# Cross-attention over 12544 keys: block maximum in two VectorE instructions, value matmuls in two halves

## The reference

```python
K = (K_in @ Wk + bk).reshape(b, l, NH, DK).transpose(0, 2, 1, 3)
V = (V_in @ Wv + bv).reshape(b, l, NH, DK).transpose(0, 2, 1, 3)
Q = (Q_in @ Wq + bq).reshape(b, lp, NH, DK).transpose(0, 2, 1, 3)
KQ = jnp.einsum('bhld,bhpd->bhlp', K, Q) / np.float32(np.sqrt(DK))
KQ = KQ + mask_pad.reshape(b, 1, l, 1)
KQ = KQ + mask_attn.T.reshape(1, 1, l, lp)
alpha = jax.nn.softmax(KQ, axis=2)
O = jnp.einsum('bhlp,bhld->bhpd', alpha, V)
O = O.transpose(0, 2, 1, 3).reshape(b, lp, NH * DK)
return O @ Wo + bo
```

## Time and profile before

| | before |
|---|---|
| median of 3 runs | 2421.47 us (2418.22 to 2424.6) |
| profiled execution | 2424.6 us |
| its span | 2422.8 us |
| granted TensorE clock over the span | 0.958 |
| TensorE matmul busy | 2268.4 us (94%) |
| weight loads busy | 1892.1 us (78%) |
| VectorE busy | 1584.7 us (65%) |
| ScalarE busy | 1504.9 us (62%) |
| GpSimd busy | 413.6 us (17%) |

### The profile page before, as it was taken

The page is one execution under the profiler, slowest core; times in us unless marked ns, Lnnn a source line. Parts: engine busy times, 40 slices in busy tenths (PEclk is TensorE's granted clock), DMA queues, the critical chain, the costliest instruction groups (busy, mean ns, idle before and its releaser), DMA issues. The chain is left out here.

```text
span 2422.8 us, 68489 instructions
## 1 busy us (share of the span) xinstructions
PE 2268.4 (94%) x26863; PEld 1892.1 (78%) x26863; DVE 1584.7 (65%) x3621; ACT 1504.9 (62%) x3044; POOL 413.6 (17%) x353
## 2 busy tenths in 40 slices
PE   7999999988999999999877999999967999999968
PEld 6888888777788788787755888888856888888758
DVE  4777777635777777777653777777735777777532
ACT  2666666634788788887523666666633666666611
POOL 3211222002221221220002122222003222212000
PEclk7999999998999999999888999999988999999969
DMA  6677666475444344341155766666517666776345
GB/s 131 116 126 126 118 115 122 61 222 149 100 118 125 99 123 115 104 119 40 46 179 117 123 107 116 116 116 117 77 52 144 121 121 121 124 125 112 49 132 173
DMA packets 152460, 279.62 MB, mean 115 GB/s; under 512 B 32829, under 2 KB 72078, under 8 KB 152218
## 3 DMA queue, kind: packets, MB, share of 16 engines
q1 hardware_dynamic: 148842, 272.18, 54.5%
q10 hardware_dynamic: 3376, 4.03, 0.7%
HBM read 120.94 MB, written 0.33 MB: 50 GB/s over the span
## 5 line engine op out<-in xcount | busy, mean ns | idle before, releaser
L1143 DVE TENSOR_REDUCE L2x_tops<-L2x_m_bank 128x1 f32<-128x448 f32 x448 | 262.5, 618 | 130.4 <-PE L2x_m_bank L907 128.2
L1143 DVE TENSOR_REDUCE L0x_tops<-L0x_m_bank 128x1 f32<-128x448 f32 x448 | 262.5, 618 | 129.7 <-PE L0x_m_bank L907 127.4
L1143 DVE TENSOR_REDUCE L3x_tops<-L3x_m_bank 128x1 f32<-128x448 f32 x448 | 262.5, 618 | 127.6 <-PE L3x_m_bank L907 125.4
L559 DVE CUSTOM_DVE_ANT_0 L1x_p_s<-L1x_p_s,L1x_mask,L1x_neg_max 128x512 f32<-128x512 f32 (+1 forms) x400 | 288.8, 743 | 57.2 <-PE L1x_p_s L320 54.7
L452 ACT ACTIVATE L1x_prob<-L1x_p_s,L1x_neg_max 128x512 f32<-128x512 f32 (+1 forms) x400 | 274.9, 687 | 68.8 <-DVE L1x_neg_max L559 66.9
L1042 ACT ACTIVATE L3x_prob<-L3x_s_bank 128x512 f32<-128x512 f32 x448 | 219.6, 542 | 90.8 <-PE L3x_s_bank L918 89.4
L1042 ACT ACTIVATE L0x_prob<-L0x_s_bank 128x512 f32<-128x512 f32 x448 | 219.6, 542 | 90.3 <-PE L0x_s_bank L918 89.2
L1042 ACT ACTIVATE L2x_prob<-L2x_s_bank 128x512 f32<-128x512 f32 x448 | 219.6, 542 | 87.8 <-PE L2x_s_bank L918 86.5
L329 PE MATMUL L1x_p_t<-net_ident,L1x_prob 128*128 128x128 f32 x1568 | 240.5, 275 | 13.7 <-ACT L1x_probT L174 11.5
L329 PEld LDWEIGHTS L1x_p_t<-net_ident,L1x_prob 128*128 128x128 f32 x1568 | 192.7, 141 | 57.1 <-ACT L1x_probT L174 23.6
L320 PE MATMUL L1x_p_s<-L1x_k_stack,L1x_q_stack 96*128 96x512 f32 (+1 forms) x400 | 182.5, 458 | 1.9 <-DVE L1x_q_stack L542 1.9
(11 more groups left out here) (766 smaller groups left out, 4469.9 us busy)
## 6 DMA issues: line engine op xcount, KB each, us to landing
L0x_k_stack<-L0x_kT SPq DMA_DIRECT2D x333, 112.0 KB, 4.1
L2x_k_stack<-L2x_kT SPq DMA_DIRECT2D x333, 112.0 KB, 4.0
L3x_k_stack<-L3x_kT SPq DMA_DIRECT2D x333, 112.0 KB, 4.0
L1x_k_stack<-L1x_kT SPq DMA_DIRECT2D x288, 128.0 KB, 2.4
L3f_w<-in_L_ffn_w SPq DMA_DIRECT2D x16, 1024.0 KB, 7.8
L0f_w<-in_L_ffn_w SPq DMA_DIRECT2D x48, 256.0 KB, 5.2
L1x_ctx<-in_ctxT SPq DMA_DIRECT2D x24, 512.0 KB, 3.9
L0x_ctx<-in_ctxT SPq DMA_DIRECT2D x13, 896.0 KB, 6.3
```

What stands on the lines that cost most here:

```text
L559: e.tensor_tensor_reduce(s, s, mask[:, odd, 0:nk], -1.0, neg_max[:, 1 - odd, h:h + 1], ALU.add, ALU.min, neg_max[:, odd, h:h + 1]).then_in ...
L1143: e.tensor_reduce(tops[:, b % 2, h, half:half + 1], m_bank[n % RING][:, 0:HALF], AX, ALU.max).then_inc(sem("m_free"), 1)
```

## The change

The block's maximum of a head is now made in two VectorE instructions. The first adds the mask in place, not negated, and reduces by maximum into a new tile `block_max`, with a constant as start value. The second, on one element per partition, waits for the first one's result, negates it and takes the minimum with the running value of the block before. It alone signals `maxed`. The exponential loses its scale of -1. Three waits per head (and one per block) that stood before the old instruction are gone, with one of its two registers.

`values` takes a half: the first half of a group's matmuls (key tiles 0 and 1 of 4) is issued nine steps behind, the second ten steps behind, in the step after. The waits stand before the first half only, and the signal `valued` is given after the second.

```diff
-VALUE_LAG = 9
+VALUE_LAGS = (9, 10)
@@ TensorE
-            def values(b, odd, g):
+            def values(b, odd, g, half):
                 nk = keys(b)
-                if g == 0:
+                nt = nk // P // 2
+                if half == 0 and g == 0:
                     e.wait_ge(sem("proj_copied"), (b + 1) * 4)
-                    if not (isinstance(b, int) and b == 0):
-                        e.wait_ge(sem("oT_copied"), b)
+                if half == 0 and g == 0 and not (isinstance(b, int) and b == 0):
+                    e.wait_ge(sem("oT_copied"), b)
                 last_of = {copied(h): h for h in range(4 * g, 4 * g + 4)}
-                for h in last_of.values():
+                for h in last_of.values() if half == 0 else ():
                     e.wait_ge(sem(copied(h)), copies(b, h))
-                for t in range(nk // P):
+                for t in range(half * nt, half * nt + nt):
...
-                i.then_inc(sem("valued"), 1)
+                if half == 1:
+                    i.then_inc(sem("valued"), 1)
...
-                at = lagging(b, odd, step, VALUE_LAG)
-                if at and at[2] % 4 == 0:
-                    values(at[0], at[1], at[2] // 4)
+                for half, lag in enumerate(VALUE_LAGS):
+                    at = lagging(b, odd, step, lag)
+                    if at and at[2] % 4 == 0:
+                        values(at[0], at[1], at[2] // 4, half)
@@ ScalarE
                     e.activation(prob[:, h % P_RING, 0:nk], p_s[h % S_RING][:, 0:nk], ACT.Exp,
-                                 bias=neg_max[:, odd, h:h + 1], scale=-1.0).then_inc(sem("exped"), 1)
+                                 bias=neg_max[:, odd, h:h + 1]).then_inc(sem("exped"), 1)
@@ VectorE
-                e.wait_ge(sem("mask_made"), b + 1)
+                if mask_kind:
+                    e.wait_ge(sem("mask_made"), b + 1)
                 for h in range(HX):
-                    made, raised = in_register(e, b * HX + h + 1), in_register(e, (b - 1) * HX + h + 1)
-                    e.wait_ge(sem("acc_zero"), 2)
-                    if not first:
-                        e.wait_ge(sem("maxed"), raised)
-                        if h == 0:
-                            e.wait_ge(sem("stepped"), b)
+                    made = in_register(e, b * HX + h + 1)
+                    if mask_kind:
+                        e.wait_ge(sem("acc_zero"), 2)
                     e.wait_ge(sem("scored"), made)
                     s = p_s[h % S_RING][:, 0:nk]
-                    e.tensor_tensor_reduce(s, s, mask[:, odd, 0:nk], -1.0, neg_max[:, 1 - odd, h:h + 1], ALU.add, ALU.min,
-                                           neg_max[:, odd, h:h + 1]).then_inc(sem("maxed"), 1)
+                    if mask_kind:
+                        e.tensor_tensor_reduce(s, s, mask[:, odd, 0:nk], 1.0, -3e38, ALU.add, ALU.max,
+                                               block_max[:, h:h + 1]).then_inc(sem("head_maxed"), 1)
+                    else:
+                        e.tensor_reduce(block_max[:, h:h + 1], s, AX, ALU.max).then_inc(sem("head_maxed"), 1)
+                    e.wait_ge(sem("head_maxed"), b * HX + h + 1)
+                    e.scalar_tensor_tensor(neg_max[:, odd, h:h + 1], block_max[:, h:h + 1], -1.0,
+                                           neg_max[:, 1 - odd, h:h + 1], ALU.mult, ALU.min).then_inc(sem("maxed"), 1)
```

More of the change, by code:

```diff
@@ L110, in cross_attention @@
     mask = sb("mask", [P, 2, KB]) if mask_kind else None
+    block_max = sb("block_max", [P, HX])
     neg_max = sb("neg_max", [P, 2, HX])
```

## The result

The changed kernel takes 2452.14 us (median of 4 runs, 2446.27 to 2457.81), the kernel before on the same chip 2419.84 (4 runs, 2413.66 to 2424.6). The ratio is 1.0135, interval 1.0108 to 1.0162: slower by 32.3 us, where +22 was forecast. It lies in the stated range, 2430 to 2461, but above the +16 to +29 that the prediction gave to its own mechanism, among the totals of its rival 2.

What follows compares the result with a forecast made beforehand. TensorE was taken to set the pace, with a chain through VectorE in B. Per block -0.21 + 0.50 + 0.64 = +0.93 us, x 24 = +22.3 us, hence 2444 us on the median; range 2430 to 2461.

Steps and rivals of the forecast that it cites:

- its own mechanism: The split and the two-part maximum lengthen TensorE's sequence: +22.3 us in all, range +16 to +29, chance 0.60.
- rival 2: VectorE becomes the bound: +1.43 us per block, +34 us in all; chance 0.15.
- -0.21 + 0.64 + a covered 0.32: Split of values, us per block: A shortens 0.21, C grows 0.64, B's added 0.32 is covered by VectorE's chain.
- A: Part of TensorE's block period from scores of head 0 to turn(1): 8.18 us before, forecast 7.97.
- C: Part of TensorE's block period from turn_out to the next block's first scores: 10.43 us before, forecast 11.07.
- +0.50 in B: In B, heads 5 and 6 each take VectorE 0.25 us longer with the maximum in two instructions.
- B: Part of TensorE's block period from turn(1) to turn_out, a chain through VectorE: 4.27 us before, forecast 4.77.
- reductions of 0.69: Sign that the prediction is wrong: VectorE's reductions fall to 0.69 us from 0.75.
- The 0.53: TensorE's wait in A before the turn of step 4, behind ScalarE's late key copy; 0.53 us per block, forecast to go.
- 1: The 0.17 us weight-load gap belongs to the wait; a group costs only 0.15 more: +11 us; chance 0.15.
- 3: Not slower: the earlier projection pays for all; with free halves A gives -0.53; -4 or +4 us total; chance 0.10.

Runs made afterwards that it cites:

- e1: The kernel before with only the values matmuls split into halves, the maximum still in one instruction: 2428.61 us, 1.0031 of the kernel before.
- e7: The changed kernel with the maximum of heads 5 and 6 made in one instruction again: 2441.6 us, 1.0071 of the kernel before.
- e8: The changed kernel with the maximum of heads 2, 3, 4 and 12 to 15 in one instruction again: 2455.43 us, 1.0127 of the kernel before.
- e5: The changed kernel with GpSimd's subtraction made in four instructions of a quarter each, nothing left out: 2445.68 us, 1.0088 of the kernel before.
- e3: The changed kernel with GpSimd's subtraction cut to 8 of 512 columns from block 3 on: 2442.91 us, 1.0119 of the kernel before.
- e4: The kernel before with the projection of key part 0 ahead of values in step 1, nothing split: 2405.18 us, 0.995 of the kernel before.

## Why the prediction was right in direction and too small

*The split, -0.21 + 0.64 + a covered 0.32.* Right. After's short block has A 7.93 and C 11.09 against 7.97 and 11.07, and e1 shows the split alone: +0.45, where these terms give 0.43.

*The two-part maximum, +0.50 in B.* Right as a path: e7 against e8 shows that the two heads in B are paid, and seven of the others are not. B measured +0.42 to +0.46, and e7 takes 0.42 off. The size was a little too large. I chose 0.66 for the hold of the reduction and kept 0.59 as a bound; it measured 0.61. So in the short block above key-low starts 0.89 after the reduction of head 5 and the output copy 0.86 after that of head 6, each against 0.66 before: +0.43 for the two, not +0.50. That a reduction comes 0.21 after a small instruction and not 0.08 does not enter B, since none follows one directly there. The prediction called reductions of 0.69 a sign against it; that sign was seen, and it meant a smaller cost and no other path. The waits that the edit removes were rightly put at nothing, though they are fewer than the section on the change says: this call has both masks, so the wait for `acc_zero` stays, and one wait per head and one per block are gone.

*The cost left out.* The failed step is that the small instruction was priced by its neighbours on VectorE alone. What delayed it was on GpSimd. In every second block, eleven times, it is held for some 2 us, and ScalarE is late for the turn of step 4. The 0.53 that the split had removed come back as 0.74: that turn starts 1.06 after its scores (877.44 to 878.50), in the short block 0.32. A is 8.73 there (871.89 to 880.62), 0.80 longer. By the max_step periods it is 24.50 - 23.72 = 0.78, hence 11 x 0.78 = 8.6 us, and 2.6 in the first block by e5: 11.2. The forecast terms are the remaining 30.9 - 11.2 = 19.7, against 22.3 (23 steady blocks at 23.72 - 22.88 = 0.84 are 19.3). e3 cuts the hold in the eleven blocks below what they can cover, e5 in the first as well, and they give back 8.7 and 11.1. The 2.6 are the weaker part: the first block is read from one profile of each kernel, and in e7 and e8, with the whole subtraction and small instructions held for 1.60 and 1.72, it took only 22.2 and 22.1. That the total came into the range was luck in part: it was drawn wide for the totals of the rivals, and the missing 11 us had no term in it.

The trace of before had the sign of it, elsewhere, and I did not read it. In another stage:

```profile
2176.84 0.66 POOL L853 TENSOR_TENSOR L3x_acc<-L3x_acc,L3x_alpha 128x272 f32<-128x272 f32 x1 [7.54 <-ACT L3x_alpha L1054]
2176.92 0.61 DVE L1167 CAST L3x_nat<-L3x_top 128x4 fp32r<-128x4 f32 x1
```

A cast of 128x4 takes 0.61 instead of 0.16 and ends within 0.03 of GpSimd's instruction that started 0.08 before it. In the three other cross-attentions of before 57 such casts started while a GpSimd instruction ran, and 55 were held so. In before's changed stage GpSimd's subtraction ran too, and the 24 reductions that started beside it kept their length: they read one tensor from SBUF (the memory where the mask lies) and one from PSUM (the memory that matmuls write here). The new instruction reads both of its tensors from SBUF. That this makes the difference is not tried by itself, and two SBUF inputs are not needed for a hold: the cast has one.

The Trainium skill, "SBUF — State Buffer", Who interferes with whom, says that a VectorE instruction with two SBUF inputs contends with a GpSimd instruction that reads SBUF, calls the port pair that the two engines share an exclusive lock, and lets the order of issue decide who is blocked. By that rule all of the 2.17 is explained, and the trace agrees: held from 873.54 to 875.71 against an end at 875.69, and not held when it starts 0.08 earlier than GpSimd's.

*Why every second block.* A pass of the loop holds two blocks. The block that begins it has its first reduction 0.71 after max_step (872.04 to 872.75), the other 0.40 (896.56 to 896.96), so the small instruction falls behind GpSimd's start in the one and ahead of it in the other. That this is the cause was read from starts and not tried by itself. The uneven start was in before as well (0.84 and 0.54), without a cost.

*Rivals.* 1 fell with e1. 2 fell with e8. 3 was right in its first term (-0.53 is real, e4) and wrong in that halves are free.

## What to carry to other kernels

Price an added instruction by where its operands lie as well as by its size: one of 128x1 with both inputs in SBUF can be held until what GpSimd is running ends, here 2.17 us. Before splitting work to bring a late transfer forward, try the order alone: swapping two entries gave the 0.5 us per block that the split bought for 0.96. And when a total fits a rival, run the one kernel that separates them: here two fused heads against seven.

## What was not expected of the hardware

- A VectorE instruction of 128x1 took 2.17 us beside a GpSimd subtraction of 2.38 us. With the subtraction in quarters the longest was 0.73.
- Values cost TensorE 0.58 from start to next start for a row of x16 in the timeline, 1.01 for x32 and 1.88 for x64: so from 16 to 32 it adds 0.43, from 32 to 64 0.87, and some 0.15 is paid once per group (an estimate from these three), beside the gap of 0.17 in front.
- With a constant start value, scale 1 and a maximum, in place of a start value from a tensor, scale -1 and a minimum, the reduction fell from 0.75 to 0.69 us, and its hold from 0.66 to 0.61. Which of the three does it was not tried.
- After an instruction that waits for the one before it, the next start came at different distances: 0.08 for a copy or the product of accumulator and alpha, 0.11 for key-low, 0.21 for a reduction of scores. In the earlier trace rows a reduction of another kind followed after 0.08, so the cause is open.
